# Mean of squares of a Mamba block: four partial sums on TensorE replaced by GpSimd additions and one TensorE step

## What is computed

```python
y = ys.transpose(1, 0, 2, 3) + x * D[None, None, :, None]
y = y.reshape(b, L, D_INNER) * jax.nn.silu(z)
y = y * jax.lax.rsqrt(jnp.mean(y * y, axis=-1, keepdims=True) + 1e-05) * norm_w
return y @ out_w.T
```

## Time and profile before

| | us |
|---|---|
| median of 3 runs | 2753.33 |
| lowest, highest | 2752.82, 2755.61 |
| the profiled execution | 2753.77 |
| its span, first to last instruction | 2751.9 |
| granted TensorE clock, mean over the span | 0.932 |
| TensorE busy | 2165.1 (79%) |
| VectorE busy | 2142.6 (78%) |
| ScalarE busy | 1156.1 (42%) |
| GpSimd busy | 976.5 (35%) |

### The profile page before, as it was taken

One profiled execution on the slowest core, in us unless ns is written; L12 is line 12 of the kernel. 1 busy time (PEld: TensorE's weight loads), 2 busy tenths in 40 slices (PEclk: granted clock), 3 DMA queues, 4 the chain that ended last, 5 costly groups with the idle time before them and its releaser, 6 DMA issues. The chain is left out here.

```text
span 2751.9 us, 41897 instructions
## 1 busy us (share of the span) xinstructions
PE 2165.1 (79%) x16488; PEld 1463.7 (53%) x16488; DVE 2142.6 (78%) x2309; ACT 1156.1 (42%) x1846; POOL 976.5 (35%) x493
## 2 busy tenths in 40 slices
PE   8993663666666666664999977899999959999998
PEld 7873552111111111112667667677777747777776
DVE  3333996999999999995788832887888848888886
ACT  2222664444444444542222211554555434555553
POOL 1110213999999999993000000112111101111211
PEclk9996986999999999998999965999999969999999
DMA  5657421112122122102222241323232142343341
GB/s 192 228 204 134 103 42 16 19 34 41 20 35 40 19 41 35 20 18 81 69 78 82 76 151 43 94 63 66 76 79 63 40 113 62 83 107 80 77 104 36
DMA packets 331134, 204.15 MB, mean 74 GB/s; under 512 B 235472, under 2 KB 312784, under 8 KB 326352
## 3 DMA queue, kind: packets, MB, share of 16 engines
q1 hardware_dynamic: 322256, 168.17, 25.5%
q0 software_dynamic: 8704, 33.56, 3.1%
HBM read 133.76 MB, written 67.90 MB: 73 GB/s over the span
## 5 line engine op out<-in xcount | busy, mean ns | idle before, releaser
L548 DVE TENSOR_TENSOR tri_av<-att,tri_v2ps 128x2816 f32<-128x2816 f32 x256 | 768.9, 3081 | 53.8 <-ACT tri_v2ps L597 47.7
L548 POOL TENSOR_TENSOR tri_av<-att,tri_v2sb 128x1280 f32<-128x1280 f32 x256 | 746.8, 2930 | 57.8 <-PE tri_bank L577 29.9
L577 PE MATMUL tri_bank<-tri_av,tri_w 128*32 128x512 f32 x4096 | 506.7, 613 | 305.4 <-DVE tri_av L548 302.2
L577 PEld LDWEIGHTS tri_bank<-tri_av,tri_w 128*32 128x32 f32 x4096 | 130.3, 111 | 681.1 <-ACT tri_ev L618 362.6
L618 ACT ACTIVATE tri_ev<-tri_bank 128x512 f32<-128x512 f32 x512 | 302.5, 597 | 418.8 <-PE tri_bank L577 378.7
L1462 DVE SCALAR_TENSOR_TENSOR mv_cv<-mv_bank,mv_cw,mv_cv 128x504 f32<-128x504 f32 (+2 forms) x240 | 171.5, 731 | 71.2 <-ACT mv_cv L1297 68.5
L1462 DVE SCALAR_TENSOR_TENSOR mh_cv<-mh_bank,mh_cw,mh_cv 128x504 f32<-128x504 f32 (+2 forms) x240 | 171.5, 731 | 71.2 <-ACT mh_cv L1297 68.5
L1104 POOL TENSOR_TENSOR mh_rstd<-mh_ms,mh_neghalf 128x4 f32<-128x4 f32 x16 | 16.1, 1009 | 392.5 <-DVE mh_ms L1506 392.5
L1104 POOL TENSOR_TENSOR mv_rstd<-mv_ms,mv_neghalf 128x4 f32<-128x4 f32 x16 | 16.1, 1008 | 388.3 <-DVE mv_ms L1506 388.3
L396 PE MATMUL smx_bank<-smx_kb,smx_q 64*64 64x128 f32 x1024 | 73.7, 304 | 80.9 <-DMA smx_kb<-qk_t 62.5
L1179 PE MATMUL mh_bank<-mh_xT_hi,mh_win_hi 128*128 128x512 f32 x288 | 120.4, 418 | 16.9 <-DVE mh_cv L1462 15.3
(11 more groups left out here) (234 smaller groups left out, 4288.5 us busy)
## 6 DMA issues: line engine op xcount, KB each, us to landing
qk_t<-prj_qk POOLq DMA_DIRECT2D x16, 1024.0 KB, 6.5
v<-prj_vs POOLq DMA_DIRECT2D x16, 1024.0 KB, 4.7
mixed_t<-tri_ev SPq DMA_DIRECT2D x1024, 8.0 KB
mh_dAb<-mh_dA SPq DMA_DIRECT2D x32, 512.0 KB, 8.2
mv_dAb<-mv_dA SPq DMA_DIRECT2D x32, 512.0 KB, 6.4
mh_xin<-x SPq DMA_DIRECT2D x20, 512.0 KB, 6.0
prj_xin<-in_x SPq DMA_DIRECT2D x16, 512.0 KB, 4.5
smx_q<-qk_t SPq DMA_DIRECT2D x8, 1024.0 KB, 10.3
```

The source lines that it names most:

```text
L548: eng.tensor_tensor(av[m % 2][:, :, d0:d1, :], a.unsqueeze(2).broadcast_to((P, 2, d1 - d0, N)), v2.unsqueeze(1).broadcast_to((P, 2, d1 - d ...
L577: mm = pe.matmul(bank[i % NB][s * M:(s + 1) * M, :], w[i // WB % 2][:, i % WB, s, :], av[i // 2 % 2][:, i % 2, s * STRIP_D:(s + 1) * STRIP ...
```

## The change

GpSimd gets a new step `add_squares(k)`, ahead of `root(k)`: it adds groups 2 and 3 of `sq` to groups 0 and 1 (128 x 1024 elements), waits for that, and adds group 1 to group 0 (128 x 512). `sum_squares` on TensorE, `copy_sums` on ScalarE and the tile `ssr` go. `columns` now uses group 0 of `sq` as weights and one column of ones, which sums over the partitions and turns in one step; it waits for both additions, and stands behind all four parts of the output projection instead of between the third and the fourth. `square` waits for `columns` of the chunk before instead of for `sum_squares`.

```diff
+            def add_squares(c):
+                pool.wait_ge(squared, 2 * c + 2)
+                pool.tensor_tensor(sq[:, 0:2, :], sq[:, 0:2, :], sq[:, 2:4, :], ALU.add).then_inc(squares_added, 1)
+                pool.wait_ge(squares_added, 2 * c + 1)
+                pool.tensor_tensor(sq[:, 0, :], sq[:, 0, :], sq[:, 1, :], ALU.add).then_inc(squares_added, 1)
...
             for k in range(NCHUNK):
+                add_squares(k)
                 root(k)
...
-            def sum_squares(c):
-                pe.wait_ge(squared, 2 * c + 2)
+            def columns(c):
+                pe.wait_ge(squares_added, 2 * c + 2)
                 pe.wait_ge(xtok_copied, PAIR * min(c + 2, NCHUNK))
-                for m in range(CT):
-                    mm = pe.matmul(PR_[1][m * 32:(m + 1) * 32, :], ones[:, :], sq[:, m, :], start=True, stop=True)
-                mm.then_inc(ss_done, 1)
-
-            def columns(c):
-                pe.wait_ge(ss_copied, c + 1)
                 for t in range(TT):
-                    mm = pe.matmul(PR_[1][:, t:t + 1], ssr[:, t * P:(t + 1) * P], pick[:, :], start=True, stop=True)
+                    mm = pe.matmul(PR_[1][:, t:t + 1], sq[:, 0, t * P:(t + 1) * P], ones[:, 0:1], start=True, stop=True)
                 mm.then_inc(col_done, 1)
...
                 if k >= 0:
                     project(k, 0)
                     project(k, 1)
-                    sum_squares(k)
                     project(k, 2)
+                    project(k, 3)
                     columns(k)
-                    project(k, 3)
...
             def square(c, half):
-                need(act, ss_done, c)
+                need(act, col_done, c)
                 act.wait_ge(gated, 2 * c + half + 1)
...
-            def copy_sums(c):
-                act.wait_ge(ss_done, c + 1)
-                need(act, col_done, c)
-                act.activation(ssr[:, :], PR_[1][:, :], ACT.Copy).then_inc(ss_copied, 1)
```

More of the change, by code:

```diff
@@ L917, in block_mamba @@
         y, sq = sb("y", [P, CT, CHUNK]), sb("sq", [P, CT, CHUNK])
-        ssr = sb("ssr", [P, CHUNK])
         ms, rstd = sb("ms", [P, TT]), sb("rstd", [P, TT])
@@ L963, in block_mamba @@
         y_done, y_read, gated, squared = sem("y_done"), sem("y_read"), sem("gated"), sem("squared")
-        ss_done, ss_copied, col_done, col_read, rstd_ready = (sem("ss_done"), sem("ss_copied"), sem("col_done"),
-                                                              sem("col_read"), sem("rstd_ready"))
+        squares_added, col_done, col_read, rstd_ready = (sem("squares_added"), sem("col_done"), sem("col_read"),
+                                                         sem("rstd_ready"))
         out_done, out_read = sem("out_done"), sem("out_read")
@@ L1381, in _ @@
                     square(k, 1)
-                    copy_sums(k)
         @block.vector
```

## The result

| | before | after |
|---|---|---|
| median, us | 2753.07 (4 runs) | 2784.46 (4 runs) |
| lowest, highest | 2752.13, 2755.61 | 2782.91, 2788.75 |
| ratio, 95% interval | | 1.0115 [1.0098, 1.0133] |
| the profiled execution, its span | 2753.77, 2751.9 | 2783.86, 2782.2 |
| granted TensorE clock | 0.932 | 0.921 |

The change costs 31 us. The forecast had the sign, and GpSimd and VectorE hold each other as it said, but it had 9 us for the size, and its range ended at 2780.

What follows compares the result with a forecast made beforehand. TensorE was taken to bound each chunk. 28 x 0.2 + 2 x 1.2 + 2 x 0.6 = +9.2 us took the profiled 2753.77 to 2763.0, so a median of 2762.5, range 2744 to 2780.

Steps and rivals of the forecast that it cites:

- What bounds the kernel: In a chunk of 29.87 to 29.90 us, TensorE, busy for 29.06, sets the time; VectorE has 3.79 us idle to give.
- What TensorE gives up: From mid output projection to the next input projection: 5.54 us become 3.46 plus 0.79, so 1.29 us less a chunk.
- Whether a scan is held: VectorE's scans beside GpSimd's additions: each waits for the rest of the other's running instruction; chance 0.58 with one addition at a time.
- the one path: VectorE's scans and GpSimd's additions: both engines share one path for SBUF reads, so GpSimd also waits for a running scan.
- The signs that the prediction named: Profile after: TensorE gap about 1.4 us ahead of `columns`, half the scans held, maximum near 2.9, VectorE idle about 1.8.
- The sum for a chunk: Chunks 0 to 13 of each block, with both holds: +0.2 us each, bounds -0.16 and +0.66.
- Slower still: Longer additions or a late mean stall the input projection's second group, or the clock falls: about 2800; chance 0.08.
- The ends: Last two chunks of each block: chunk 14 +1.2 us, chunk 15 +0.6 us.
- two additions in a row: Rival: GpSimd does both additions before the held scan; -0.25 to -0.3 us a chunk, 2750.5; chance 0.12.
- The whole gain: Rival: scans don't clash with GpSimd, or don't hold it; -1.29 us a chunk arrives, 2719.4; chance 0.22.

## Why the prediction was right or wrong

**What bounds the kernel** was right: the times of all kernels here follow what TensorE does or waits for between the output projection and the second group of the input projection.

**What TensorE gives up**: 1.29 forecast, 1.19 measured without additions. The output projection and `columns` came out as put: the chain of waits of that run has them with 6.91 and 0.79 us. The missing 0.1 lies behind them, in the first group of the next input projection:

```profile
2549.22 6.91 PE mv_bank L1237 x32
2556.12 0.79 PE mv_bank L1246 x8
2556.91 1.52 PE mv_bank L1184 x6
```

Behind `columns` that group takes 1.52 us, behind the output projection it took 1.41. The sum for a chunk has 0.07 for this change of matmul, the 1.29 has nothing. In the changed kernel, behind the wait of 1.27 us, `columns` takes 1.05 us, not 0.79.

**Whether a scan is held** was the step chosen from one row of another instruction, L474, and it held in both directions: scans to 2.74 us, additions from 2.35 to 3.27 and from 1.27 to 2.07. For GpSimd behind a running scan no row of before had a number: that wait was my choice between two bounds, and the one path that the forecast has both engines share was an assumption that no run shows. The runs show the times: 0.92 and 0.80 us of waiting in the two additions, and scans of at most 1220 ns beside fills that only write. The signs that the prediction named came too: a gap of 1.27 us on TensorE (1.4 forecast), half of the scans held, the longest 2.74 us (2.9), and VectorE idle for 2.07 us ahead of the first tap (1.8).

**The sum for a chunk**, +0.2 forecast with bounds of -0.16 and +0.66: +0.33 measured where the clock stays up. The wait is 0.14 us shorter than the 1.41 I had, and `columns` 0.26 longer than its 0.79, which makes the 0.12 that the sum is short. The additions by themselves take 2.35 and 1.27 us against my 2.27 and 1.13; their 3.62 lie above the upper bound of 3.52 that I took from products at least as long as 512 elements. They don't make the wait longer, because a held addition ends sooner behind the scan than it would alone: the smaller one 1.07 us behind (2507.23 to 2508.30), for which I had 1.13.

**The step that failed** is the sentence in the rival *Slower still* that gave a lower clock from the added wait little weight and no price. I compared with a chunk of 31.1 us in which the clock stayed at 1.00. I hadn't looked at how that chunk waits: its longest idle stretch is 1.09 us, among the transposes. And the 0.57 at the end of a block, behind a wait of 2.44 us, I took for something apart. The runs put the loss at about 1.1 us in one chunk of two, some 14 us of the 31, caused by TensorE's wait ahead of `columns`: gone when the wait is filled, there when the wait comes from fills alone. Whether the thinly used time of `columns` behind the wait takes part in it wasn't tested apart, and why the clock falls in one chunk and not in the next, behind the same wait, stays open. Without the loss the changed kernel would be at 2770, as the run with work in the wait is, and inside the range.

**The ends** came out as forecast. The root of a chunk stands 9.68 us behind the start of its output projection instead of 7.60, the interval from the root of chunk 13 to that of chunk 14 is 0.7 us shorter, and the next one 0.6 longer in both blocks. That is 2.0 us for a block and 4.0 for both; I had 3.6 and 0.2 for each of the two chunks that the 26 intervals leave out. The rest of the 4.1 us ahead of the first root of `mv` is 2.0 more from the start of that block to its first output projection, where the low clock fell. In `mh` the same stretch took 1.8 us less than before. That the two nearly cancel is luck.

**The rivals**: two additions in a row were put at 2750.5, and the run with one long addition, which stands in for them, took 2740. There the mean starts 2.85 us behind the end of the output projection (2563.16 and 2566.01), where I had 3.3, since nothing lies between two additions that are one and the held scan runs on at once; `scale_out` then doesn't wait for the root. Half a microsecond in 28 chunks makes about the difference. The whole gain was put at 2719.4; the run with fills gave 2724.8 and the one without additions 2730.0. *Slower still* had 0.08, and its price came from longer additions and a late mean; the measured 2784 lies in its region, but for the reason that it named last.

## What to carry to other kernels

A step moved to an idle engine was not free here where its reads met another engine's two-operand reads: scans of 1.22 us took up to 2.74, and additions of 2.35 and 1.27 us took 3.27 and 2.07. Look at what the other engine does in exactly that stretch, and count the wait of each for the other, one instruction at a time. If a wait on TensorE can't be avoided, put independent matmuls of the next stage in front of the waiting ones: here that turned a loss of 31 us into a gain of 27 to 28. And price a new idle stretch on TensorE at either clock, not just by its length: here one of 1.27 us was followed by 3.4 us at a clock of 0.50 in 13 of 26 chunks, about 1.1 us each.

## What the runs showed of the hardware

The clock fell to 0.50 for 3.4 us behind an idle stretch of 1.27 us followed by eight one-column matmul records, in 13 of 26 chunks, and in 10 of 26 behind one of 1.41; behind one of 0.83 us at the same place it fell in none. In the kernel before, a wait of 1.09 us among the transposes left it at 1.00, and one of 3.39 us at the start of `mh`, ahead of the fourth group of the input projection, took it to about 0.5 as well.

The length of the idle stretch alone doesn't decide. Ahead of the last product for `y`, in one chunk of `mh`, TensorE stood idle for 1.12 us in the run with work in the wait, and the clock fell; in the second run with `columns` inside the input projection it stood idle for 1.61 us there, and the clock stayed (first the one, then the other, each with a window behind the stretch):

```profile
1943.01 0.27 PE L1227 MATMUL mh_bank<-mh_S,mh_xtok 64*64 64x64 f32 x1 [1.12 <-issue]
...
1944.00:1946.00 2.00, 2.00 (x11) 2.00 (x10) 1.80 (x3) 1.19 (x2) 0.00 (x0) 0.50 0.00 0
...
2048.91 0.27 PE L1236 MATMUL mh_bank<-mh_S,mh_xtok 64*64 64x64 f32 x1 [1.61 <-issue]
...
2049.00:2051.00 2.00, 2.00 (x17) 1.75 (x17) 1.93 (x4) 1.14 (x3) 0.00 (x0) 1.00 0.00 0
```

What tells these cases apart wasn't tried.

GpSimd's additions of two operands took 1268, 2349 and 3432 ns for 512, 1024 and 1536 elements when nothing held them, and its fills of 1024 elements 951 ns.
